# Softmax denominators inverted in place as a 512-column row, not as a 32x16 square

## The reference

```python
xs = reshape(group_norm(x), (B, T, C))            # B 16, T 1024 tokens, C 512, 32 groups
q, k, v = xs @ Wq[h], xs @ Wk[h], xs @ Wv[h]      # 8 heads of 64 columns
att = softmax(q @ k.T / 8, axis=-1)               # 1024 x 1024 for each image and head
out = concat_heads(att @ v) @ Wproj + bproj
return x + reshape(out, x.shape)
```

## Time and profile before

| what | value |
|---|---|
| median of 3 runs | 4452.45 us (4452.08 to 4463.26) |
| the profiled execution, its own time | 4452.18 us |
| its span from first to last instruction | 4450.4 us |
| TensorE matmul busy (PE) | 4410.9 us, 99% |
| TensorE weight load busy (PEld) | 3611.6 us, 81% |
| ScalarE busy (ACT) | 2952.8 us, 66% |
| GpSimd busy (POOL) | 2857.7 us, 64% |
| VectorE busy (DVE) | 2580.5 us, 58% |
| DMA engines, mean over the span | 48 GB/s |
| granted TensorE clock, mean | 0.999 of full speed |

### The profile page before, as it was taken

How to read it: one execution, slowest core, us unless ns; L and a number is a source line. 1 busy time by engine, 2 the same in 40 slices (tenths; PEclk the granted TensorE clock), 3 DMA queues, 4 the chain that set the end, 5 groups by cost and what they waited for, 6 DMA issues and landing times.

```text
span 4450.4 us, 61770 instructions
## 1 busy us (share of the span) xinstructions
PE 4410.9 (99%) x20864; PEld 3611.6 (81%) x20864; DVE 2580.5 (58%) x5063; ACT 2952.8 (66%) x5644; POOL 2857.7 (64%) x2227
## 2 busy tenths in 40 slices
PE   8999999999999999999999999999999999999999
PEld 7888888888888888888888888887888888888886
DVE  6655646556465565655656556565664656646454
ACT  5766757667576675756757567575775757757575
POOL 5666666666666566665666656666666666567566
PEclk9999999999999999999999999999999999999999
DMA  3111121211111112111121111211112111121201
GB/s 78 38 53 49 37 61 34 57 45 38 59 37 58 43 35 64 36 60 39 33 70 35 56 39 34 68 38 55 38 33 68 39 57 36 36 66 38 59 25 56
DMA packets 156825, 211.42 MB, mean 48 GB/s; under 512 B 56544, under 2 KB 57568, under 8 KB 156512
## 3 DMA queue, kind: packets, MB, share of 16 engines
q1 hardware_dynamic: 156512, 207.47, 16.5%
HBM read 105.12 MB, written 34.08 MB: 31 GB/s over the span
## 4 chain that ended last, share of the span: by engine, by line
PE 94%; DVE 2%; POOL 1%; ACT 1%; DMA 1%; issue 0%; SPq 0%; POOLq 0%; ACTq 0%; DVEq 0%
PE bank L663 16%; PE bank L715 10%; PE bank L881 10%; PE bank L882 10%; PE bank L883 10%; PE bank L709 10%; PE bank L708 10%; PE bank L675 8%; PE bank L693 8%; PE bank L681 1%; POOL prob_l L1294 1%; PE bank L700 1%; DVE smax L1106 1%; DVE xs L1073 0%; ACT prob L899 0%
## 5 line engine op out<-in xcount | busy, mean ns | idle before, releaser
L1294 POOL TENSOR_TENSOR prob_l<-prob,prob_h 128x512 fp32r<-128x512 f32 x1660 | 2140.5, 1297 | 1437.9 <-ACT prob_h L899 1418.2
L1106 DVE TENSOR_REDUCE smax<-bank 128x1 f32<-128x512 f32 x2048 | 1347.5, 682 | 868.2 <-PE bank L715 864.1
L899 ACT ACTIVATE prob<-bank 128x512 f32<-128x512 f32 x2048 | 1232.2, 602 | 575.3 <-PE bank L709 413.1
L899 ACT ACTIVATE prob_h<-bank 128x512 fp32r<-128x512 f32 x2048 | 1227.2, 599 | 461.9 <-PE bank L883 393.0
L881 PE MATMUL bank<-prob_h,vh 128*128 128x512 f32 x2048 | 822.2, 401 | 7.8 <-ACT acc L1018 4.2
L708 PE MATMUL bank<-q_hh,k_hl 128*128 128x512 f32 x2048 | 813.1, 397 | 0.0
L709 PE MATMUL bank<-q_lm,k_h 65*128 65x512 f32 x2048 | 811.4, 396 | 0.0
L882 PE MATMUL bank<-prob_h,vl 128*128 128x512 f32 x2048 | 806.3, 394 | 0.0
L883 PE MATMUL bank<-prob_l,vh 128*128 128x512 f32 x2048 | 805.8, 393 | 0.0
L715 PE MATMUL bank<-k_hl,q_hh 128*128 128x512 f32 x2048 | 716.4, 402 | 6.2 <-DVE smax L1106 6.0
L881 PEld LDWEIGHTS bank<-prob_h,vh 128*128 128x128 f32 x2048 | 388.8, 190 | 109.8 <-ACT acc L1018 15.4
(11 more groups left out here) (83 smaller groups left out, 5064.6 us busy)
## 6 DMA issues: line engine op xcount, KB each, us to landing
xs<-in_x SPq DMA_DIRECT2D x252, 256.0 KB, 2.8
q_hh<-q_hh SPq DMA_DIRECT2D x256, 128.0 KB, 2.2
k_hl<-k_h SPq DMA_DIRECT2D x256, 128.0 KB, 2.3
inv_b<-inv_dram SPq DMA_DIRECT2D x256, 128.0 KB, 2.8
out_x<-xs SPq DMA_DIRECT2D x128, 256.0 KB, 2.0
q_lm<-q_lm SPq DMA_DIRECT2D x256, 2.0 KB
den<-acc SPq DMA_DIRECT2D x256, 2.0 KB, 1.7
inv_dram<-inv SPq DMA_DIRECT2D x256, 2.0 KB, 1.4
```

Source lines behind the costliest of these rows:

```text
L899: return nc.scalar.activation(out, ps[ST + bank][:, :], ACT.Exp, scale=SCALE)
L1106: nc.vector.tensor_reduce(smax[:, 2 * t + half:2 * t + half + 1], ps[SM + turn][:, :], AX.X, ALU.max).then_inc(rows_used, 1)
L1294: nc.gpsimd.tensor_tensor(prob_l[:, r3, :], prob[:, ring2, :], prob_h[:, r3, :].bitcast(F32), ALU.subtract).then_inc(prob_l_pool, 1)
```

## The change

The square and its transfer go: `den`, `inv`, the semaphore `den_in` and `den_to_square` with its three calls. VectorE waits for `acc_ready` itself and inverts the denominators where they lie in `acc`, 512 columns, into the partitions of `inv_b` that the half does not use as its broadcast rows. For even heads this is one partition (64); for odd heads, whose denominators lie in partition 63, the instruction takes the band of partitions 32 to 63, of which the last is used. `inv_to_rows` writes that one partition to `inv_dram` and then broadcasts as before. The slots of the remaining parts are the same.

```diff
-        den = sb("den", [32, 16])
-        inv = sb("inv", [32, 16])
...
-        den_in = sem("den_in")
...
-            def den_to_square(s, ahead, tc):
-
-                sp.wait_ge(acc_ready, s.heads(2, ahead, tc + 1))
-                r = rows(s.h + ahead)[1]
-                sp.dma_start(den[:, :], acc[r:r + 1, tc, :]).then_inc(den_in, 16)
-
             def inv_to_rows(s, ahead, tc):
 
                 sp.wait_ge(inv_ready, s.heads(2, ahead, tc + 1))
-                sp.dma_start(inv_dram[0:1, :].rearrange("a (p f) -> (a p) f", p=32), inv[:, :]).then_inc(inv_out, 16)
+                r = rows(s.h + ahead)[1]
+                sp.dma_start(inv_dram[0:1, :], inv_b[r:r + 1, :]).then_inc(inv_out, 16)
                 sp.wait_ge(inv_out, s.heads(32, ahead, 16 * (tc + 1)))
                 sp.dma_start(inv_b[rows(s.h + ahead)[0], :],
                              inv_dram[0, :].partition_broadcast(D)).then_inc(inv_in, 16)
...
-                    if i == s.den_slots[1] and not first:
-                        den_to_square(s, -1, 1)
...
-                    if i == s.den_slots[0]:
-                        den_to_square(s, 0, 0)
...
-            den_to_square(s, -1, 1)
             inv_to_rows(s, -1, 1)
...
                     dve.wait_ge(o_ready, s.heads(2, ahead, tc))
-                dve.wait_ge(den_in, s.heads(32, ahead, 16 * (tc + 1)))
-                nc.vector.reciprocal(inv[:, :], den[:, :]).then_inc(inv_ready, 1)
+                dve.wait_ge(acc_ready, s.heads(2, ahead, tc + 1))
+                band = slice(D, D + 1) if (s.h + ahead) % 2 == 0 else slice(D // 2, D)
+                nc.vector.reciprocal(inv_b[band, :], acc[band, tc, :]).then_inc(inv_ready, 1)
```

## The result

| | before | after |
|---|---|---|
| median of 4 runs | 4452.26 us | 4948.85 us (4945.95 to 4952.31) |
| ratio, with its 95% interval | | 1.1111 (1.1095 to 1.1128) |
| profiled execution / its span | 4452.18 / 4450.4 us | 4949.71 / 4947.9 us |
| TensorE matmul busy | 4410.9 us | 4597.7 us |
| VectorE busy | 2580.5 us | 3458.7 us |

The sign was right, the size was not: 4724 us was forecast, with a range up to 4850. Between the two spans lie 497.5 us; 186.8 of them are TensorE busy for longer with the same 20864 matmuls, and 310.7 are TensorE standing still.

What follows compares the result with a forecast made beforehand. TensorE's matmuls bound the kernel, so only its stops behind VectorE's 3.0 us reciprocal count: 266 + 4 + 2 = 272 us on 4452.18 gives 4724 us, 6.1% slower, range 4620 to 4850, chance 0.78.

Steps and rivals of the forecast that it cites:

- the sum: TensorE's stops behind VectorE, 17.8 us an image: 266 us for 15 images, 4 for the last, 2 at the end.
- the third rival: TensorE's granted clock halves after each of seven long stops an image: 357 us more, 5081 us; chance 0.04.
- the prediction's own signs of being wrong: Reciprocal under 0.8 or over 4 us; stops behind GpSimd's low parts; steady-stretch clock below 1; TensorE not later.
- the covers: At each of an image's 16 reciprocals on VectorE, the longest reciprocal that makes no matmul late; seven were 0.49 to 1.26 us.
- the longest stop that I forecast: At 1011.33, cover 0.49 us: with a 3.0 us reciprocal TensorE stands still for 2.51 us.
- the reductions' fixed part: VectorE's wide reciprocal priced with the reductions' 153 ns fixed: 4.9 ns a column, 2.65 us for 512.
- the fill's: High end for VectorE's wide reciprocal, fixed part at most the 85 ns fill: 9.1 ns a column, 4.76 us.
- The four free places: Four of an image's sixteen reciprocal positions, where the longer reciprocal was to cost TensorE nothing.
- the change without its width: Removed transfer: earlier start credited where VectorE waited for it, elsewhere hidden; SyncE's fewer issues and longer wait: nothing.
- GpSimd's later multiplication: Up to 2.8 us later, low parts queued behind it: put at nothing; uncovered, about 1 us at some of 96 waits.

Runs made afterwards that it cites:

- the dose: Changed kernel with the reciprocal over 256, 384 or 448 columns instead of 512: 4562.91, 4705.97 and 4812.91 us; the four traces include the 512-column one.
- the earlier transfer: Kernel before with the transfer to the square issued one slot earlier (slots 8 and 0): 4453.94 us against 4455.27, ratio 0.9998.
- the narrow variant: Changed kernel with the reciprocal over 16 columns instead of 512: 4442.10 us against 4454.43, ratio 0.9974.

## Why the prediction was wrong

**The step that failed** is the clock, which the sum put at nothing and left to the third rival with a chance of 0.04, because "here a busy engine stops for 2 us at a time". The clock did follow, behind single stops, 4 to 5 times an image, and took some 131 of the 497 us; the mean of 0.97 in the steady stretch is one of the prediction's own signs of being wrong. Without the clock, the covers at the measured 3.34 us would have given 4786 us, inside the range. I had judged from the one fall in the trace before that several pauses must come together. That trace is less clear than I took it to be: the low clock begins at 4421.14, inside one pause of 2.69 us, while the pauses of 0.80 and 1.26 us shortly before had brought none. TensorE's first matmul after that pause, and the busy times of the low stretch (columns as in rows 1):

```profile
4421.82 0.76 PE L693 MATMUL bank<-wp_h,o_h 128*128 128x512 f32 x1 [2.69 <-POOL o_l L1330]
```

```profile
4421.14:4427.97 6.83, 6.15 (x15) 4.83 (x16) 0.89 (x2) 0.76 (x2) 4.25 (x4) 0.50 0.07 22
```

One case can't tell a single long pause from several together, and no pause over 1 us stands in that trace's steady stretch; but this one pause was only a little longer than the longest stop that I forecast (2.51 us), so 0.04 was far too little. That rival and the forecast were never alternatives either: the stops bring the falls, and the sum should have carried them as a term with bounds (nothing to 357 us).

**The term that was mis-sized** is the reciprocal: 3.34 us, not 3.0. Between the reductions' fixed part (2.65) and the fill's (4.76) the truth lay further up than I leaned. Three widths give 6.25 ns a column, and 3343 - 512 x 6.25 = 143 ns fixed; the 16-column square's 231 ns would leave 131 by the same slope, and 16 columns of the row, at 243 ns, leave 143 again. (In the prediction, 10 ns less of fixed part add 0.31 us, not 0.32; nothing hangs on it.) The same covers at 3.34 us give 21.9 us an image, 334 in all, so this term is worth 62 us. The Trainium skill, VectorE: DVE Perf Modes, "Walkthrough: the 8-slice pipeline in each mode", names a repeat count of 8 for this iterated divide. The runs show 6.25 ns, as an estimate six cycles at that page's 0.96 GHz, so the eight cycles a column that the prediction estimated from that count are not what it costs.

**Right:** what bounds the kernel, and who waits for what. The covers were read from the trace before and met the trace after closely. Position by position (numbered through an image), TensorE's pauses after against the covers' stops at 3.34 us: position 5, 2.64 (2.65); position 7, 2.92 (2.85); position 9, 0.48 (0.49); position 14, 2.74 (2.54); position 15, 2.55 (2.85). The four free places stayed free but for 0.14 us at one; among them is the one before which VectorE had waited 2.47 us for the transfer. Off were the places with transfer or statistics in the chain: position 11, 1.92 (2.19), position 12, 3.78 (2.81), since a second stop behind VectorE's late `xl` adds 0.59, and position 13, 1.19 (2.08). In all 20.9 us of pauses an image, of which 0.9 were there before, against 21.9 by the covers; counted from start to start, as the covers are, the stops cost 22.7 us an image more than before.

**Also off:** the change without its width is worth some 12 us, not nothing; under a wide reciprocal they are not to be seen. GpSimd's later multiplication cost what I gave it, nothing that shows: no TensorE wait for `prob_l` is among the large ones.

## What to carry to other kernels

For this reciprocal the columns decide the cost, not the numbers inverted: the same 512 are 0.23 us as a square of 32 rows and 3.34 us as one row, and a 1.7 us transfer for which TensorE does not wait is a cheap price for the square. Before putting a long instruction into a full engine's queue, read at each place how long the queue may be held until the bounding engine needs what stands behind it; that reading held within some 10% in total, with single places off by up to 1 us; check the room of the whole stretch too. When a change makes TensorE stop for about 2 us or more, add the low clock after each stop as a term of the sum, with bounds.

## What the runs showed of the hardware that was not expected

A single stop of 1.6 us or more in an otherwise busy TensorE can be followed by 3.41 or 6.8 us at half clock; of stops of 2.6 us and more 58 of 60 were in the four traces of the dose, and 69 of 79 with the wide reciprocal in the kernel before. The fall often begins only when TensorE is working again: in those four traces 91 of 136 low stretches began up to 1.8 us after the stop had ended, the others inside it (in the stop shown, which ends at 1088.53, at 1088.44). VectorE's reciprocal costs 6.25 ns a column, six times a reduction's 1.03, and takes 3.34 us on 1 partition as on 32. And a token normalisation on VectorE takes 0.55 us where GpSimd's subtraction starts 0.10 to 0.25 us after it, and some 1.6 us where that starts 0.01 to 0.07 us after it (the first normalisation of head 6's step in the traces of the kernel before, the earlier transfer and the narrow variant).
